# A fused attention and LoRA layer: scaling the context by the softmax sums instead of the probabilities, with the inverse sums spread through HBM

## The reference

```python
q = hidden_states @ Wq + bq                     # (2, 512, 4096); k and v: (2, 512, 1024)
q, k = _rope(q, pos), _rope(k, pos)
scores = jnp.einsum('bgrsd,bgtd->bgrst', qg, k) / jnp.sqrt(D)
scores = jnp.where(causal, scores, finfo.min)
probs = jax.nn.softmax(scores, axis=-1)
ctx = jnp.einsum('bgrst,bgtd->bgrsd', probs, v)
attn = ctx.reshape(B, S, H * D) @ Wo + bo
x = _layernorm(x + attn)
x = _layernorm(x + ffn(x))                      # dense + LoRA experts weighted by a router softmax
```

## Time and profile before

| | |
|---|---|
| median of 3 runs | 845.27 us (844.85 to 846.61) |
| the profiled execution, span | 844.5 us |
| PE matmul busy | 812.5 us, 96% |
| PE weight load busy | 695.8 us, 82% (beside the matmuls) |
| DVE busy | 584.2 us, 69% |
| ACT busy | 514.6 us, 61% |
| POOL busy | 344.2 us, 41% |
| granted TensorE clock, mean | 0.996 |

### The profile page before, as it was taken

One profiled execution on the slowest core, in us unless ns is written; L12 is line 12 of the kernel. 1 busy time (PEld: TensorE's weight loads), 2 busy tenths in 40 slices (PEclk: granted clock), 3 DMA queues, 4 the chain that ended last, 5 costly groups with the idle time before them and its releaser, 6 DMA issues.

```text
span 844.5 us, 14449 instructions
## 1 busy us (share of the span) xinstructions
PE 812.5 (96%) x4361; PEld 695.8 (82%) x4361; DVE 584.2 (69%) x1547; ACT 514.6 (61%) x1254; POOL 344.2 (41%) x311
## 2 busy tenths in 40 slices
PE   7789999999999999999999999999999999999986
PEld 6677888888888888888888888888888888887875
DVE  4776767666776767666776767666776767688657
ACT  5767756666666756666666756666666766664210
POOL 4435643354334533354334533354334533240415
PEclk9999999999999999999999999999999999999999
DMA  9201000020101010010101010020101011000002
GB/s 292 63 1 63 14 26 25 1 64 14 50 0 60 15 36 14 0 62 12 50 0 61 13 37 13 0 62 12 50 0 50 0 41 35 1 15 1 1 0 101
DMA packets 27693, 28.56 MB, mean 34 GB/s; under 512 B 3664, under 2 KB 20224, under 8 KB 27664
## 3 DMA queue, kind: packets, MB, share of 16 engines
q1 hardware_dynamic: 27664, 28.20, 10.5%
HBM read 26.10 MB, written 2.10 MB: 33 GB/s over the span
## 4 chain that ended last, share of the span: by engine, by line
issue 45%; POOL 22%; PE 21%; DVE 9%; ACT 2%; DMA 1%; SPq 1%; POOLq 1%; DVEq 0%; ACTq 0%
POOL rope_rot L612 9%; POOL q_lo L589 4%; POOL wq_lo L589 3%; PE ps_proj L272 3%; PE ps_proj L270 3%; PE ps_proj L271 3%; POOL wo_lo L589 2%; PE ps_tr L1063 2%; DVE prob L850 2%; POOL wkv_lo L589 2%; DVE prob L807 1%; DVE rope_cos L766 1%; PE ps_sc L270 1%; PE ps_out L270 1%; PE ps_out L272 1%
## 5 line engine op out<-in xcount | busy, mean ns | idle before, releaser
L807 DVE CUSTOM_DVE_ANT_0 prob<-ps_sc,mask_sb 128x256 f32<-128x256 f32 (+3 forms) x256 | 115.1, 487 | 126.1 <-PE ps_sc L1108 72.3
L483 ACT ACTIVATE prob<-prob,negmax 128x256 f32<-128x256 f32 (+3 forms) x256 | 141.4, 556 | 72.6 <-DVE negmax L807 72.5
L612 POOL TENSOR_TENSOR rope_rot<-rope_rot,sin_sb 128x512 f32<-128x512 f32 x77 | 100.0, 1299 | 195.6 <-ACT rope_rot L420 195.6
L589 POOL TENSOR_TENSOR q_lo<-rope_cos,q_hi 128x512 fp32r<-128x512 f32 x64 | 85.8, 1340 | 193.2 <-ACT q_hi L436 193.2
L418 ACT ACTIVATE rope_rot<-ps_proj,bias_cols 64x512 f32<-64x512 f32 x80 | 54.7, 684 | 127.8 <-PE ps_proj L272 127.4
L850 DVE TENSOR_SCALAR prob<-prob,rinv 128x128 f32<-128x128 f32 (+3 forms) x256 | 117.9, 503 | 4.5
L738 DVE TENSOR_TENSOR pT_lo<-ps_tr,pT_hi 128x384 fp32r<-128x384 f32 (+2 forms) x192 | 100.4, 549 | 8.1 <-ACT pT_hi L459 6.5
L270 PE MATMUL ps_proj<-xT_hi,wq_hi 128*128 128x512 f32 x256 | 105.9, 414 | 0.0
L1063 PE MATMUL ps_tr<-ident,prob 128*128 128x128 f32 x640 | 93.5, 275 | 12.0 <-DVE prob L850 11.5
L738 DVE TENSOR_TENSOR ctx_lo<-ps_ctx,ctx_hi 128x512 fp32r<-128x512 f32 x64 | 44.2, 690 | 83.3 <-ACT ctx_hi L452 83.3
L272 PE MATMUL ps_proj<-xT_hi,wq_lo 128*128 128x512 f32 x256 | 100.8, 394 | 0.0
(11 more groups left out here) (195 smaller groups left out, 1833.4 us busy)
## 6 DMA issues: line engine op xcount, KB each, us to landing
wq_raw<-in_attn_Wq SPq DMA_DIRECT2D x16, 512.0 KB, 4.7
wo_raw<-in_attn_Wo SPq DMA_DIRECT2D x8, 1024.0 KB, 5.4
wk_raw<-in_attn_Wk SPq DMA_DIRECT2D x8, 256.0 KB, 5.2
wv_raw<-in_attn_Wv SPq DMA_DIRECT2D x8, 256.0 KB, 2.7
out<-acc SPq DMA_DIRECT2D x8, 256.0 KB, 2.0
acc<-in_attn_hidden_states SPq DMA_DIRECT2D x4, 256.0 KB, 4.1
acc<-in_attn_hidden_states SPq DMA_DIRECT2D x1, 1024.0 KB, 8.9
wq_raw<-in_ffn_W_base SPq DMA_DIRECT2D x1, 1024.0 KB, 5.4
```

What stands on the lines that cost most here:

```text
L483: return act.activation(prob[:, slot, SCOL[i]:SCOL[i + 1]], prob[:, slot, SCOL[i]:SCOL[i + 1]], ACT.Exp, bias=negmax[:, slot, i:i + 1], sc ...
L589: return pool.tensor_tensor(dst, full, high.bitcast(F32), ALU.subtract)
L612: pool.tensor_tensor(rope_rot[:, slot, :], rope_rot[:, slot, :], sin_sb[:], ALU.mult).then_inc(sin_done, 1)
L807: return nc.vector.tensor_tensor_reduce(out=prob[:, slot, SCOL[i]:SCOL[i + 1]], in0=ps_sc[bank][:, at:at + w], in1=mask_sb[:, S - w:S], sc ...
```

## The change

- Probabilities are no longer multiplied; PE's transposes wait for the exponentials (`exp_done`) instead of `p_ready`. The reciprocal is one instruction for all four row tiles.
- SP has a new function `spread_rinv`. In each step it waits for the reciprocal of the next head, writes rinv (128 partitions by 4) to a buffer in HBM, waits for that write and until DVE has used the row before it (`ctx_f_d`), and reads it back as one row of 512 numbers spread over all 128 partitions (rinv_row, one buffer).
- DVE multiplies ps_ctx by this row into a new tile ctx_f in SBUF, as its first work of a step; it reads rinv_row with a stride of four floats. ctx_hi (ACT) and ctx_lo (DVE) now read ctx_f, and both stand behind the copies and subtractions of pT.
- PE's matmuls into ps_ctx wait for `ctx_f_d` instead of `ctx_lo_d`.
- To make room, wk and wv share a buffer, the bias rows lie in ctx_f, and lora_B is loaded into a part of wo_raw. SP's loop is written by steps, with the loads of the weights at n = 0, 1, 4 and 6; at the start the load of the first wv waits for `wk_lo_d`, and all loads behind it with it.

The diff without the renamed buffers in the lines of ACT and POOL and the names of semaphores:

```diff
@@ -131,6 +131,7 @@
+    rinv_dram = nc.dram_tensor("rinv_dram", (2, P, TT), F32, kind="Internal").ap()
     ctx = ExitStack()
@@ -147,8 +148,7 @@
         wq_raw = sb("wq_raw", [P, KT, R * D])
-        wk_raw = sb("wk_raw", [P, KT, D])
-        wv_raw = sb("wv_raw", [P, KT, D])
+        wkv_raw = sb("wkv_raw", [P, KT, D])
         wo_raw = sb("wo_raw", [P, R, HID])
@@ -177,12 +177,13 @@
         ident = sb("ident", [P, P])
-        bias_rows = sb("bias_rows", [H + 2 * G, D])
         bias_cols = sb("bias_cols", [P, H + 2 * G])
         row_bias = sb("row_bias", [P, HID])
         negmax = sb("negmax", [P, 2, TT])
         rowsum = sb("rowsum", [P, 2, TT])
         rinv = sb("rinv", [P, 2, TT])
+        rinv_row = sb("rinv_row", [P, P, TT])
+        ctx_f = sb("ctx_f", [P, S])
         ids_sb = sb("ids_sb", [P, E])
@@ -197,7 +198,8 @@
-        wb_raw, la_raw, lb_raw = wq_raw, wk_raw, wv_raw
+        wb_raw, la_raw, lb_raw = wq_raw, wkv_raw, wo_raw[:, 1, :]
+        bias_rows = ctx_f[0:H + 2 * G, 0:D]
         wbT_hi = wq_hi[:].rearrange("p r k d -> p r (k d)")
...
@@ -315,14 +318,15 @@
                 if i == 0:
-                    sp.dma_start(wk_raw[:], wk_v[:, :, 0:D]).then_inc(wk_in, 16)
+                    sp.dma_start(wkv_raw[:], wk_v[:, :, 0:D]).then_inc(wk_in, 16)
             sp.dma_start(bias_rows[0:H, :], bq.rearrange("(h d) -> h d", d=D)).then_inc(bias_in, 16)
             sp.dma_start(bias_rows[H:H + G, :], bk.rearrange("(h d) -> h d", d=D)).then_inc(bias_in, 16)
             sp.dma_start(bias_rows[H + G:H + 2 * G, :], bv.rearrange("(h d) -> h d", d=D)).then_inc(bias_in, 16)
             wq_half(0, slice(0, half))
             sp.dma_start(cos_sb[:], cos_t).then_inc(rope_in, 16)
             sp.dma_start(sin_sb[:], sin_t).then_inc(rope_in, 16)
-            sp.dma_start(wv_raw[:], wv_v[:, :, 0:D]).then_inc(wv_in, 16)
+            sp.wait_ge(wk_lo_d, 1)
+            sp.dma_start(wkv_raw[:], wv_v[:, :, 0:D]).then_inc(wv_in, 16)
             sp.dma_start(row_bias[:], bo.partition_broadcast(P)).then_inc(bo_in, 16)
@@ -332,26 +336,56 @@
-            with sp.Fori(1, G) as g:
-                sp.wait_ge(wk_lo_d, g)
-                sp.dma_start(wk_raw[:], wk_v[:, :, bass.ds(g * D, D)]).then_inc(wk_in, 16)
-                sp.wait_ge(wv_lo_d, g)
-                sp.dma_start(wv_raw[:], wv_v[:, :, bass.ds(g * D, D)]).then_inc(wv_in, 16)
-                sp.wait_ge(wq_lo_d, g * R)
-                wq_half(0, bass.ds(g * (R * D), half))
-                wq_half(1, bass.ds(g * (R * D) + half, half))
-                sp.wait_ge(wo_lo_d, g * R)
-                sp.dma_start(wo_raw[:], wo_v[:, bass.ds(g * R, R), :]).then_inc(wo_in, 16)
+            def spread_rinv(g, n):
+
+                k = g * STEPS + n + 1
+                slot = (n + 1) % 2
+                wait(sp, rinv_done, k + 1)
+                sp.dma_start(rinv_dram[slot], rinv[:, slot, :]).then_inc(rinv_out, 16)
+                wait(sp, rinv_out, 16 * k + 16)
+                wait(sp, ctx_f_d, k)
+                sp.dma_start(rinv_row[:].rearrange("p q t -> p (q t)"),
+                             rinv_dram[slot].rearrange("q t -> (q t)").partition_broadcast(P)).then_inc(row_in, 16)
+
+            def step(g, n):
+
+                prev, cur, nxt = has(g)
+                if cur and n == 0:
+                    wait(sp, wv_lo_d, g + 1)
+                    if nxt:
+                        sp.dma_start(wkv_raw[:], wk_v[:, :, bass.ds(g * D + D, D)]).then_inc(wk_in, 16)
+                if cur and nxt and n == 1:
+                    wait(sp, wq_lo_d, g * R + R)
+                    wq_half(0, bass.ds(g * (R * D) + R * D, half))
+                    wq_half(1, bass.ds(g * (R * D) + (R * D + half), half))
+                if cur and nxt and n == 4:
+                    wait(sp, wk_lo_d, g + 2)
+                    sp.dma_start(wkv_raw[:], wv_v[:, :, bass.ds(g * D + D, D)]).then_inc(wv_in, 16)
+                if cur and nxt and n == 6:
+                    wait(sp, wo_lo_d, g * R + R)
+                    sp.dma_start(wo_raw[:], wo_v[:, bass.ds(g * R + R, R), :]).then_inc(wo_in, 16)
+                if cur if n < 7 else nxt:
+                    spread_rinv(g, n)
+
+            step(-1, 7)
+            for n in range(STEPS):
+                step(0, n)
+            with sp.Fori(1, G - 1) as g:
+                for n in range(STEPS):
+                    step(g, n)
             sp.wait_ge(wq_lo_d, G * R)
             sp.dma_start(wb_raw[:], w_base.rearrange("(t p) h -> p t h", p=P)).then_inc(wb_in, 16)
-            sp.wait_ge(wk_lo_d, G)
+            sp.wait_ge(wv_lo_d, G)
             sp.dma_start(la_raw[:].rearrange("p k d -> p (k d)"), lora_a.rearrange("e r h -> (e r) h")).then_inc(la_in, 16)
-            sp.wait_ge(wv_lo_d, G)
-            sp.dma_start(lb_raw[:].rearrange("p k d -> p (k d)").rearrange("p (e c) -> p e c", e=E),
+            for n in range(4):
+                step(G - 1, n)
+            sp.wait_ge(wo_lo_d, G * R)
+            sp.dma_start(lb_raw.rearrange("p (e c) -> p e c", e=E),
                          lora_b.rearrange("e (p j) r -> p e (j r)", j=4)).then_inc(lb_in, 16)
-            sp.wait_ge(wo_lo_d, G * R)
             sp.dma_start(rt_raw, router_w).then_inc(rt_in, 16)
+            for n in range(4, STEPS - 1):
+                step(G - 1, n)
             sp.wait_ge(acc_init, NT)
...
@@ -442,14 +476,6 @@
                 prev, cur, nxt = has(g)
-
-                if (cur if n else prev):
-                    N, m = g * STEPS + (n - 1), (n - 1) % STEPS
-                    b, h = m // R, m % R
-                    wait(act, pv_done, N + 1)
-                    if h == 0:
-                        wait(act, wo_done, g * STEPS - (STEPS - TT) if b == 0 else g * STEPS)
-                    act.activation(ctx_hi[:, b, h, :], ps_ctx[:], ACT.Copy).then_inc(ctx_hi_d, 1)
@@ -459,6 +485,13 @@
                     act.activation(pT_hi[:, PT_T0:PT_T2], ps_tr[TR_P[n] % 2][:], ACT.Copy).then_inc(tr_hi_d, 1)
+                if (cur if n else prev):
+                    N, m = g * STEPS + (n - 1), (n - 1) % STEPS
+                    b, h = m // R, m % R
+                    wait(act, ctx_f_d, N + 1)
+                    if h == 0:
+                        wait(act, wo_done, g * STEPS - (STEPS - TT) if b == 0 else g * STEPS)
+                    act.activation(ctx_hi[:, b, h, :], ctx_f[:], ACT.Copy).then_inc(ctx_hi_d, 1)
                 if isinstance(g, int) and g == 0 and n == 0:
...
@@ -774,9 +807,12 @@
                 if (cur if n else prev):
-                    m = (n - 1) % STEPS
-                    wait(dve, ctx_hi_d, N)
-                    low(ctx_lo[:, m // R, m % R, :], ps_ctx[:], ctx_hi[:, m // R, m % R, :]).then_inc(ctx_lo_d, 1)
+                    wait(dve, pv_done, N)
+                    wait(dve, row_in, 16 * g * STEPS + 16 * n)
+                    wait(dve, ctx_lo_d, N - 1)
+                    nc.vector.tensor_tensor(ctx_f[:].rearrange("p (t q) -> p t q", t=TT),
+                                            ps_ctx[:].rearrange("p (t q) -> p t q", t=TT),
+                                            rinv_row[:].rearrange("p q t -> p t q"), ALU.mult).then_inc(ctx_f_d, 1)
@@ -784,6 +820,10 @@
                     low(pT_lo[:, PT_T0:PT_T2], ps_tr[TR_P[n] % 2][:], pT_hi[:, PT_T0:PT_T2]).then_inc(tr_lo_d, 1)
+                if (cur if n else prev):
+                    m = (n - 1) % STEPS
+                    wait(dve, ctx_hi_d, N)
+                    low(ctx_lo[:, m // R, m % R, :], ctx_f[:], ctx_hi[:, m // R, m % R, :]).then_inc(ctx_lo_d, 1)
@@ -842,15 +882,8 @@
                 if has_s:
-                    for part, (i0, i1) in enumerate(((0, TT - 1), (TT - 1, TT))):
-                        wait(dve, exp_done, 2 * N + 3 + part)
-                        nc.vector.reciprocal(rinv[:, slot, i0:i1], rowsum[:, slot, i0:i1]).then_inc(rinv_done, 1)
-                        wait(dve, rinv_done, 2 * N + 3 + part)
-                        for i in range(i0, i1):
-                            last = nc.vector.tensor_scalar(prob[:, slot, SCOL[i]:SCOL[i + 1]],
-                                                           prob[:, slot, SCOL[i]:SCOL[i + 1]],
-                                                           rinv[:, slot, i:i + 1], None, ALU.mult)
-                    last.then_inc(p_ready, 1)
+                    wait(dve, exp_done, 2 * N + 4)
+                    nc.vector.reciprocal(rinv[:, slot, :], rowsum[:, slot, :]).then_inc(rinv_done, 1)
                 for k in (*preps(g, n, 1), *preps(g, n, 2)):
@@ -1064,7 +1097,7 @@
                     tr_free(g, j)
-                    wait(pe, p_ready, g * STEPS + (n + 1))
+                    wait(pe, exp_done, 2 * g * STEPS + 2 * (n + 1))
                     p_tile(3, 3, 0, (1 + j) % 2)
@@ -1150,7 +1183,7 @@
                     N, b = g * STEPS + n, n // R
-                    wait(pe, ctx_lo_d, N)
+                    wait(pe, ctx_f_d, N)
```

(13 more changed lines are left out.)

## The result

The changed kernel takes 839.2 us (median of 4 runs, 837.17 to 841.3), the kernel before, run beside it, 845.94 (844.85 to 846.66). The ratio is 0.9918, with a 95% interval of 0.9897 to 0.9939: faster, in the range of 837 to 847, and further down than the 841.8 forecast. The profiled execution has a span of 836.4 us against 844.5, so 8.1 us have to be accounted for where the sum has 3.45. The medians are 6.7 us apart: the four executions of the changed kernel have spans of 836.4, 835.4, 839.5 and 838.4 us at mean granted clocks of 0.996, 0.998, 0.994 and 0.994, and the profiled one is not a slow one of them.

The account below looks back on a forecast made before the run. PE was taken as the bound, busy 812.5 of 844.5 us. The terms -13.2 + 1.6 + 6.3 + 0.5 + 1.35 = -3.45 gave 841.1, and 841.8 with the runs' median 0.8 above the profile; range 837 to 847.

Parts of the forecast that it names:

- Gain: Starts of steps: PE's 19 waits for DVE's multiply of the probabilities go, saving 13.2 us, at least 8.
- The deduction for step 0: First step: 1.3 us taken off the saving, since the second half of its transposes also needs v_lo.
- n = 1: Eight steps with a K tile: one more DVE operation before the score masks, 0.2 us each, 1.6 us lost.
- n = 5: Seven steps with a K tile: POOL blocks ctx_lo's two SBUF inputs, PE 0.9 us late each, 6.3 us lost.
- Start: Shared wk and wv buffer holds back wv's load and those behind it: 0.5 us lost, range 0 to 2.1.
- End: Last head: ctx_f and ctx_hi now precede ctx_lo, so PE's wait grows by 1.35 us, range 0 to 2.
- No cost for the DMAs and SP: Each step: rinv's write and read land with 7 us to spare, and delayed weight loads cost nothing.
- ctx_f at 0.69: DVE's new multiply at each step's start, taken at 690 ns from the nearest row, despite its strided operand.
- A: Steps with n = 5: ctx_lo isn't blocked or PE doesn't feel it; 6.3 becomes 1.4 to 1.8, 837 us; 20%.
- B: First steps' gains don't hold, or the start costs 2.1: takes back 1.6 to 5.5 us, 843.4 to 847; 16%.
- C: Steps with n = 1: POOL's sine meets ctx_lo there too, 5.6 us more, 847.4, slower; 12%.
- D: Every step: rinv's round trip outlasts a step, from 13 us on; up to 63 us per us beyond, 900 us; 4%.

Follow-up runs that it names:

- experiment 1: The kernel before with the softmax scaling left out altogether, neither probabilities nor context divided by the sums: 833.37 us, ratio 0.9846.
- experiment 2: The changed kernel with ctx_lo computed from PSUM (ps_ctx) again, PE waiting for it before reusing the bank: 835.01 us, ratio 0.9867.
- experiment 3: The changed kernel with ctx_lo moved behind the reciprocal in the steps with n = 1 and n = 5: 834.41 us, ratio 0.9854.
- experiment 5: Experiment 3 with the router's constants right after the last ctx_f, and the last addition and statistics behind ctx_lo: 832.65 us, ratio 0.984.
- experiment 7: Experiment 3 with the rinv row read from HBM twice, one after the other: 834.8 us in one run.
- experiment 4: The changed kernel with rinv written to HBM transposed, so ctx_f reads its row without a stride: 912.76 us, ratio 1.0769.
- experiment 6: Experiment 3 with ctx_f walking the row in order, and PSUM and the output at a stride: 834.42 us in one run.

## Why the prediction came out as it did

The direction and the mechanism were right, and the time is inside the range. But 841.8 was to be the centre of the likeliest case's 840 to 843.5, and the result is 839.2. By the medians the change gave -6.7 us, in the profiled executions -8.1, where the sum says -3.45. Term by term, by the profiles:

- **Gain, 13.2 predicted, 14.5 measured** (experiment 1, and 14.7 with the first step of the changed kernel). Of the 13.2, some 4.7 were for steps 0, 2, 4 and 6, 7.1 for the thirteen waits, 0.3 for a wait of 0.18 in n = 5 of group 7, and 1.2 for step 62. Experiment 1 measures 3.5, 7.9 (0.60 each, where length plus 0.16 gives 0.54 on the average), 0.4 and 1.4. The deduction for step 0 was right: it gains nothing in experiment 1 and 0.2 in the changed kernel. It should have been made for step 4 too, which gave 0.8 of the 1.7 counted, since the second half of its transposes now waits 0.78 for v_lo (third set of rows below). What was missing is 0.1 us in each of steps 0 and 4 in seven groups, 1.3 in all. There the trace of before has no wait but eight transposes that stretch over 1.16 us, in the changed kernel 1.04 (third set). I had read only the bracketed waits. A likely cause, which no run isolates, is v_lo: before, it starts at 406.42, when the last multiply ends; now DVE has nothing in front of it.
- **n = 1, +1.6 predicted, +0.5 measured.** This term was mis-sized, and most of what was measured is something else. The queueing that it priced at 0.2 a step costs nothing beyond 0.02 us in groups 1 to 6 and 0.1 in group 7. Its working took DVE's idle time of 0.26 as all the slack there is, and PE's tolerance as none: the masks come 0.13 later there and PE hardly at all. The other 0.42 comes once, in group 0, where ctx_lo starts inside POOL's multiply by the sine and takes 1.19 us. PE's wait for negmax behind it is 0.62 us, and 0.21 in experiment 2, where ctx_lo has one input in PSUM (second set of rows below).
- **n = 5, +6.3 predicted, +5.0 measured**: 0.51 in group 0 and 0.73 to 0.77 in six steps, beside experiment 1. The mechanism is shown by experiment 2; ctx_lo's end, 0.55 after POOL's, is as in the earlier trace rows. The masks come 0.86 us later (5.47 us after the last matmul into ps_ctx instead of 4.61) and PE absorbs 0.1 of it, about what it absorbs in n = 1. Of the 1.3 between forecast and measurement 0.4 is group 0, and the rest some 0.15 in each of the six others, where the masks were to come 0.93 later and PE was to absorb nothing.
- **Start, +0.5 predicted, nothing measured.** wv's load is issued 2.2 us later, as worked out from the earlier trace rows, and ACT starts on it no later at all (12.45 before), as the first two rows of the first set show. PE's wait for x of batch 1 grew from 0.52 to 2.02 us, but a wait of 1.00 for q_lo behind it went. The first step ends at 42.22 us, before at 42.46. In experiments 2, 3, 5 and 7, whose start is the changed kernel's, it ends at 42.33 to 42.65, so tenths of this are chance.
- **End, +1.35 predicted, +1.3 measured.** PE's wait for ctx_lo went from 0.21 to 1.76 (its third row), 1.55 us, of which 0.25 is made up later. That the sum came out is partly luck: ctx_f, counted at 0.6 to 0.7 us, stands in this chain with 1.05, and what PE makes up later was not counted.
- **No cost for the DMAs and SP: right** (experiments 4 and 7 give it its bounds). A write and a read take 1.4 and 3.3 us; I had 2.7 each. From the issue of the write to the landing of the row it is 7.0 us by the median, since the read also waits until ctx_f has used the row before it.
- **ctx_f at 0.69: wrong, it takes 1.10**, as some of its operands have a stride. None of the 64 steps of PE feels it; in the chain at the end it is some 0.4 of the 1.55 us (an estimate, 1.05 less 0.69). DVE's busy time fell by 39 us (584.2 to 545.1) and not by the forecast 75: of the 36 between, 64 x (1.10 - 0.65) = 29 are ctx_f's stride, and 10 the ctx_lo that is held up in 24 places (54.7 us in all, where before it took 44.2), less 3 of roundings and overlaps.

The changed kernel's rows for the start and the end (first set), from SP's, ACT's and PE's timelines:
```profile
8.96 0.38 SPq L329 DMA_DIRECT2D wkv_raw<-in_attn_Wv  x1
...
12.11 0.63 ACT L422 ACTIVATE wkv_hi<-wkv_raw 128x512 fp32r<-128x512 f32 x1 [1.24 <-DMA wkv_raw<-in_attn_Wv]
...
773.08 0.50 PE L273 MATMUL ps_sc<-wo_hi,ctx_hi 128*128 128x512 f32 x1 [1.76 <-DVE ctx_lo L771]
```

Second set: n = 1 of group 0, from DVE's, POOL's and PE's timelines of the changed kernel, and PE's row in experiment 2:
```profile
44.55 1.19 DVE L771 TENSOR_TENSOR ctx_lo<-ctx_f,ctx_hi 128x512 fp32r<-128x512 f32 x1
...
43.89 1.30 POOL L645 TENSOR_TENSOR rope_rot<-rope_rot,sin_sb 128x512 f32<-128x512 f32 x1
...
47.81 0.50 PE L273 MATMUL ps_sc<-k_hi,q_hi 128*128 128x512 f32 x1 [0.62 <-DVE negmax L847]
```
```profile
47.83 0.50 PE L273 MATMUL ps_sc<-k_hi,q_hi 128*128 128x512 f32 x1 [0.21 <-DVE negmax L847]
```

Third set: the second four transposes in step 4 of group 0, changed; then the eight transposes in a later step with n = 4, before (with v_lo) and changed:
```profile
72.09 0.66 PE L1096 MATMUL ps_tr<-ident,prob 128*128 128x128 f32 x4 [0.78 <-DVE v_lo L771]
```
```profile
406.42 0.68 DVE L738 TENSOR_TENSOR v_lo<-ps_tr,v_hi 128x512 fp32r<-128x512 f32 x1
...
406.66 1.16 PE L1063 MATMUL ps_tr<-ident,prob 128*128 128x128 f32 x8
```
```profile
401.82 1.04 PE L1096 MATMUL ps_tr<-ident,prob 128*128 128x128 f32 x8
```
The two DMAs of the changed kernel (count, KB, median us from issue to landing):
```profile
rinv_row<-rinv_dram SPq DMA_DIRECT2D x64, 256.0 KB, 3.3
rinv_dram<-rinv SPq DMA_DIRECT2D x64, 2.0 KB, 1.4
```

Together: -14.7 + 0.5 + 5.0 + 1.3 = -7.9, of the -8.1 measured. The 4.5 us between this and the forecast are 1.5 in the gain, 1.1 in n = 1, 1.3 in n = 5 and 0.5 at the start: no step that the sum rests on fell, four sizes were set too carefully, all to the same side. By the medians it is 6.7 - 3.45 = 3.2 us; the 1.3 between lie within the 4 us by which the four executions of the changed kernel differ.

Of the rivals, A's time (837) was close, but its mechanism is refuted: ctx_lo is blocked and PE feels it. B didn't come: the first steps lost only part of their gains. C came once in eight: in n = 1 the sine meets ctx_lo in group 0 alone, which is the 0.42 us above. D is real, but only with a round trip beyond the 13 us of its condition: 15.1 in experiment 4, and 7.0 here, of which 4.7 are the two transfers.

## What to carry to other kernels

When a wait is taken away by moving work, price the removal alone by a kernel that leaves the work out: here it was 14.5 us, the change kept 9.4, and one displaced SBUF-only subtraction, moved to a place where POOL is idle, gave the rest back. An operation whose inputs move from PSUM to SBUF changes more than its duration; look at what POOL does at that moment. In a queue with idle time, place the operation with the latest consumer last.

## What the runs showed of the hardware

- DVE's subtraction of two SBUF tiles (128x512, fp32r output) takes 0.66 to 0.69 us alone. Started while a POOL operation on SBUF tiles is running, it takes up to 1.41 and ends 0.55 us after that one, in 24 of 24 places; with one input in PSUM it stays at 0.67 to 0.69 us in all 64 steps. In 16 of the 24 places the next POOL operation starts before the subtraction ends, and takes 1.73 to 1.75 us instead of 1.30.
- A DVE multiply of 128x512 with operands of which some are read at a stride takes 1.10 us, with all in order 0.69, whichever operands have the stride.
- A write of 2 KB to HBM takes 1.4 us as 128 pieces of 16 bytes; as 512 pieces of 4 the read that waits for it is issued 7.9 to 12.4 us after it.
- After the wait of 1.76 us at the end, three kernels (experiments 2, 3 and 7) ran some 3.4 us at half the clock; the changed kernel and experiment 6, with nearly the same wait, didn't. Later in the tail PE waits 2.15 to 2.24 us for xT_lo, and a stretch of half clock begins within 1.5 us of the end of that wait in all of these traces, and in those of the kernel before and of experiment 1; in experiment 5 the same wait has none. What decides it stays open. In experiment 4, where ctx_f waits for the row 46 times and PE 19 times for pT_lo behind it (47.4 us), the mean granted clock is 0.966; in the changed kernel it is 0.996.
